# Later takers for the edge counts, one piece of keys per group, and a weight low half ahead of the keys

## What is computed

```python
xn = layernorm(x)
# gnn, two layers; deg_inv = 1 / max(number of edges into a node, 1)
agg = segment_sum(h[src], dst)                       # both layers
h   = relu(xn @ W_self0 + deg_inv * agg(xn) @ W_neigh0 + b0)
gnn = h @ W_self1 + deg_inv * agg(h) @ W_neigh1 + b1
# mix: a linear attention over all nodes
Q, K = elu(xn @ Wq + bq) + 1, elu(xn @ Wk + bk) + 1
KV   = sum(K * (xn @ Wv + bv)); Ksum = sum(K)
mix  = gelu((Q * KV / (Q * Ksum + 1e-6)) @ Wo + bo)
x = x + gnn + mix
x = x + ffn(layernorm(x))                            # quantised, weights (384, 1024)
```

## Time and profile before

| | |
|---|---|
| time, median of 3 runs | 1212.84 us (1212.08 to 1213.51) |
| profiled execution, its own time | 1213.64 us |
| span in its trace | 1211.8 us |
| PE busy | 1157.4 us, 96% |
| DVE busy | 679.4 us, 56% |
| ACT busy | 356.5 us, 29% |
| POOL busy | 393.2 us, 32% |
| scattering indirect DMAs | 160, 2160 ns each on POOL |
| mean granted TensorE clock | 0.986 |

### The profile page before, as it was taken

How to read it: one execution, slowest core, us unless ns; L and a number is a source line. 1 busy time by engine, 2 the same in 40 slices (tenths; PEclk the granted TensorE clock), 3 DMA queues, 4 the chain that set the end, 5 groups by cost and what they waited for, 6 DMA issues and landing times.

```text
span 1211.8 us, 15245 instructions
## 1 busy us (share of the span) xinstructions
PE 1157.4 (96%) x6309; PEld 622.7 (51%) x6309; DVE 679.4 (56%) x1232; ACT 356.5 (29%) x446; POOL 393.2 (32%) x224
## 2 busy tenths in 40 slices
PE   4898999999999999995999999999999999999978
PEld 3554555555555554442444555444444445569934
DVE  7766947658475563335633444656564345582763
ACT  5634333333324323310521112222210012251640
POOL 1266767758677684677400000000000000000000
PEclk8999999999999999998999999999999999999989
DMA  9935344353442439532731034432220080000005
GB/s 259 339 81 140 65 100 99 71 135 50 103 85 37 98 71 311 128 53 58 271 109 39 22 116 162 127 105 88 87 87 35 18 156 1 1 1 1 2 8 161
DMA packets 156151, 117.61 MB, mean 97 GB/s; under 512 B 93401, under 2 KB 132569, under 8 KB 155058
## 3 DMA queue, kind: packets, MB, share of 16 engines
q1 hardware_dynamic: 86744, 103.41, 27.4%
q0 software_dynamic: 69024, 13.07, 8.4%
q10 hardware_dynamic: 314, 0.16, 0.0%
HBM read 90.13 MB, written 21.41 MB: 92 GB/s over the span
## 4 chain that ended last, share of the span: by engine, by line
PE 50%; DMA 21%; issue 14%; POOL 12%; DVE 2%; ACT 1%; SPq 0%; POOLq 0%; ACTq 0%; DVEq 0%
PE ps L1053 25%; DMA at_scratch<-copies,cell 18%; POOL at_scratch L598 12%; PE ps L1085 7%; PE ps L1114 6%; PE ps L1151 6%; PE ps L1181 3%; DMA at_scratch<-zeros 2%; DMA raw<-in_L_mix_Wk_dram 1%; PE ps L1123 1%; PE ps L1101 1%; PE ps L991 0%; DMA parts<-at_scratch 0%; POOL at_scratch L588 0%; DMA key_scratch<-key_r 0%
## 5 line engine op out<-in xcount | busy, mean ns | idle before, releaser
L598 POOL DMA_INDIRECT at_scratch<-copies,cell x160 | 345.6, 2160 | 173.6 <-DMA at_scratch<-copies,cell 93.7
L983 PE MATMUL ps<-xnT,whl 128*128 128x512 f16 (+1 forms) x2160 | 383.3, 340 | 0.0
L983 PEld LDWEIGHTS ps<-xnT,whl 128*128 128x128 f16 x2160 | 211.1, 98 | 169.9 <-issue 1.7
L1053 PE MATMUL ps<-hb,hT 128*128 128x512 f16 x960 | 207.7, 379 | 1.3 <-DVE hT L1516 1.3
L1053 PEld LDWEIGHTS ps<-hb,hT 128*128 128x128 f16 x960 | 93.9, 98 | 114.5 <-DVE hT L1516 1.8
L1053 PE MATMUL ps<-hb,xnT 128*128 128x512 f16 x480 | 105.9, 383 | 12.4 <-DVE hb L1386 12.4
L579 POOL PARTITION_ALL_REDUCE ag_fw<-am_fw x9 | 3.2, 354 | 317.0 <-DVE am_fw L1399 317.0
L1053 PE MATMUL ps<-hb,VT 128*128 128x512 f16 x480 | 103.9, 379 | 1.5 <-ACT S_b L740 1.5
L1085 PE MATMUL ps<-AT,P 125*128 125x512 f16 (+1 forms) x480 | 84.7, 339 | 0.0
L1053 PEld LDWEIGHTS ps<-hb,xnT 128*128 128x128 f16 x480 | 47.3, 99 | 69.9 <-DVE hb L1386 12.9
L1114 PE MATMUL ps<-P,AT 125*128 125x512 f16 x360 | 79.0, 379 | 0.0
(11 more groups left out here) (231 smaller groups left out, 1190.1 us busy)
## 6 DMA issues: line engine op xcount, KB each, us to landing
raw<-in_L_gnn_W_neigh_dram SPq DMA_DIRECT2D x32, 512.0 KB, 5.0
raw<-in_L_gnn_W_self_dram SPq DMA_DIRECT2D x24, 512.0 KB, 5.2
key_b<-key_scratch SPq DMA_DIRECT2D x8, 1250.0 KB, 8.8
raw<-in_L_mix_Wo_dram SPq DMA_DIRECT2D x16, 512.0 KB, 3.9
parts<-at_scratch POOLq DMA_DIRECT2D x20, 312.5 KB, 3.8
at_scratch<-zeros POOLq DMA_DIRECT2D x6, 1020.0 KB, 17.7
x_all<-in_x_dram SPq DMA_DIRECT2D x9, 512.0 KB
x_acc<-in_x_dram SPq DMA_DIRECT2D x9, 512.0 KB
```

The lines of the kernel that those rows point to most:

```text
L598: pool.indirect_dma_start(out=at_scr[c % 2][:, :], out_offset=bass.IndirectOffsetOnAxis(ap=cell[:, c:c + 1], axis=0), in_=copies[:, c:c + ...
L983: mm = pe.matmul(acc_of(c)[:, a:b], whl[:, i, wp, k, :], xnT[:, k, ap, a:b], start=(k == 0 and wp == 0 and ap == 0), stop=(k == KC - 1 and ...
L1053: mm = pe.matmul(half_bank(i), stationary[:, k, ap, t * TP:t * TP + P], hb[:, n % 2, k, wp, :], start=(k == 0 and wp == 0 and ap == 0), st ...
```

## The change

Four places. `PIECE_AT` was (1, 2) for group 0 and then one piece, g + 2, for groups 1 to 5; now group g prepares piece g + 1, for groups 0 to 6. The low half of the fourth chunk of the next group (`chunk_lo(g + 1, 3)`) stood behind the keys and now stands ahead of them. The ten counts were behind tiles 15, 17, 19, 21, 23, 25, 27, 29, 30 and 31 and are now behind 21, 22, 24, 25, 27, 28, 30, 31, 33 and 34. `DEG_TILE` goes from 33 to 36.

```diff
-    PIECE_AT = [(1, 2)] + [(g + 2,) if g + 2 < NPC else () for g in range(1, KC)]
+    PIECE_AT = [(g + 1,) if g + 1 < NPC else () for g in range(KC)]
...
-        DEG_TILE = 33
+        DEG_TILE = 36
...
-        PART_TILE = {i: s for s, i in enumerate((15, 17, 19, 21, 23, 25, 27, 29, 30, 31))}
+        PART_TILE = {i: s for s, i in enumerate((21, 22, 24, 25, 27, 28, 30, 31, 33, 34))}
...
                 v_low(g)
+                if g + 1 < KC:
+                    chunk_lo(g + 1, 3)
                 for p in PIECE_AT[g]:
                     cells(p)
-                if g + 1 < KC:
-                    chunk_lo(g + 1, 3)
-                else:
+                if g + 1 == KC:
                     for j in range(4):
                         job(("half", WO_, 1, j))
```

## The result

| | before | changed |
|---|---|---|
| median | 1212.59 us (4 runs, 1212.08 to 1213.51) | 1199.38 us (4 runs, 1197.6 to 1199.69) |
| ratio | | 0.9887, 95% interval 0.987 to 0.9904 |
| profiled execution, own time | 1213.64 us | 1197.6 us |
| span | 1211.8 us | 1195.8 us |

1.1% faster. Later batches timed the kernel before more often: medians 1213.3 (21 runs, 1209.1 to 1218.4), 1212.6 (11 runs), 1214.4 (13 runs, 1199.4 to 1218.3) and 1212.7 (17 runs, 1205.3 to 1219.8). Of the 11 runs ten lie between 1206.0 and 1215.4 and one, with its clock granted at 0.943 of full speed instead of 0.98 to 0.99, at 1239.98. So the kernel before scatters by 9 us and more, and one of its runs was as fast as the changed kernel; the changed kernel's five runs lie within 2.2 us. The interval above comes from four runs of before that happened to lie within 1.5 us, and is narrower than that scatter allows.

The account below looks back on a forecast made before the run. PE, busy 96% of the span, was taken as the bound, others mattering only where it waits. -7.3 - 14.0 + 6.05 = -15.25 us against 1213.64 gave 1198.4, forecast as 1198.0 (median 0.8 lower), range 1195.0 to 1203.0.

Parts of the forecast that it names:

- The short wait: PE's wait behind chunk 5 for squares of group 2, 5.78 us plus 1.54 slower clock: 7.3 us, all gained.
- The long wait: PE's 12.41 us wait in tile 20 for a low half, plus 1.6 slower clock: 14.0 us, all gained.
- -7.3 - 14.0: Gains behind chunk 5 and in tile 20, added as two separate terms of the sum.
- Pieces later, cost 0: Keys prepared one group later: POOL never stands for keys, its margin of 9 us grows; costed at 0.
- The scatters end as before: POOL's scatters keep their times although keys come later; parts there since 558.75.
- DVE held by POOL: POOL's first six additions, 557 to 571, slow DVE; a count taken at 10.40 us, low halves at 5.04.
- the 9 us of room: DVE frees tile 23 at 588, PE asks at 596.8: holds by 9 us in the worst sum.
- rival B: New wait in tiles 26 to 36 from late banks, tenth count or degree read: 1199 to 1205, chance 0.12.
- The reciprocal, 6.05 us: After tile 39, PE waits 4.55 us for the reciprocal behind tile 38, plus 1.5 slower clock: cost 6.05.
- The clock term: PE's slower clock after the wait for the reciprocal: 1.5 us taken, bounds 0 and 1.7.
- Rival C: Slower: first count waits for later scatters, PE waits from tile 28 if parts land after 579; 1214 or more, chance 0.02.

Follow-up runs that it names:

- experiment 3: Changed kernel with the low half of the fourth chunk back behind the keys, group 0 still with one piece: 1199.41 us.
- Experiment 4: Changed kernel with the old table of pieces of keys (two in group 0), the low half still ahead of them: 1199.46 us.
- experiment 2: Kernel before with only the counts moved to tiles 21 to 34 and DEG_TILE 36: 1206.32 us, ratio 0.9942.
- experiment 7: Kernel before with 100 small memsets on POOL between the last scatter and the first read of the parts: 1231.47 us, ratio 1.0179.
- experiment 8: Changed kernel with 100 small memsets on POOL ahead of the read of the parts: 1199.43 us, ratio 0.9902.
- experiment 10: Kernel before with only the low half of the fourth chunk ahead of the keys, pieces and counts as before: 1209.24 us, ratio 0.9969.
- experiment 1: Changed kernel with counts and DEG_TILE back in their old places, so only keys and low half are moved: 1201.34 us, ratio 0.9918.
- experiment 9: Changed kernel with 200 memsets on POOL ahead of the parts: 1215.3 us; also the changed kernel again, 1199.81, and the kernel before again, 1209.36.
- experiment 5: Changed kernel with every count one tile earlier and DEG_TILE 35: 1191.85 us, ratio 0.9835.
- experiment 6: Changed kernel with the reciprocal in two, 1024 columns behind tile 36 and 226 behind tile 38: 1191.75 us, ratio 0.9832.

## Why the prediction was right, and where its reasoning was not

**The forecast.** 1198.0, likeliest case 1196 to 1200; 1199.38 was measured, and each sign that it named is there: no wait at the sums behind chunk 5, squares ready at 107.1 (forecast "near 108"), no wait in tile 20, one new wait for the reciprocal of 4.53 (4.55).

**The short wait.** Mechanism as argued: the slot of chunk (1,3). Experiments 3 and 4 add that the two edits each suffice; the prediction gave neither by itself a price. Its size of 5.78 was that of one trace: the others that have it show 3.90, 3.99 and 4.87.

**The long wait.** DVE's stand behind tile 15 held tile 20, as experiments 2, 7 and 8 show. But "-7.3 - 14.0" as two gains side by side is wrong for the kernel before, and only right because the change makes both edits. There the path ran through the scatters: the time was the start of the read behind them plus 659 us. The first page said so, in its part on the chain that ended last, with 30% for the scatters and their DMAs; the prediction does not use that part and went by PE's waits alone. A change of group 0 alone would have been forecast 7.3 us faster. The order alone (experiment 10) gives 3.5 and keys and order together (experiment 1) 12.0, both through an earlier end of the scatters. Next to experiment 1 the later counts add only 2 us at the median, for they pay 7.6 at the reciprocal; what they add besides is that the time no longer follows the scatters.

**Pieces later, cost 0.** POOL waited for keys at no scatter after the first, right. "The scatters end as before" was wrong: in the ten traces of kernels without the wait behind chunk 5 they end early enough for a read of the parts at 540 to 555, in the four with it at 550 to 563. The two ranges overlap, so it is the medians of experiments 1 and 10 that carry this. It cost the forecast nothing, since with the counts in their new places PE does not wait for the scatters' end.

**DVE held by POOL.** The dearest low half was given 5.04 us and the dearest count 10.40. Experiment 4 has one of 8.38, the repeat of the changed kernel one of 8.54, and experiment 2 one of 12.34:

```profile
567.80 12.34 DVE L1386 SCALAR_TENSOR_TENSOR hb<-raw,sw,hb 128x1024 f16<-128x1024 f32 x1 [0.35 <-ACT hb L705]
```

The first counts of experiments 8 and 9 took 12.93 and 12.50. So both bounds were too low, and the 9 us of room were less than stated; with parts up to 18 us late none of it reached PE, as experiment 8 shows. Of the Trainium skill's rule (page "SBUF — State Buffer", section "Who interferes with whom"), that the second to issue blocks until the first finishes, the exclusion is borne out, the length is not: a VectorE instruction stood behind five or six GpSimd additions in a row (10.40, 12.34, 12.50, 12.93 us, one addition being 2.3).

**The margins of rival B.** The tenth count and the degree read were said to hold by 1.1 and 0.8 us. They held in every trace; in the changed kernel's first the count was done 1.3 us and the read 0.9 us before PE's column sums began.

**The reciprocal, 6.05 us.** The wait was right to 0.02 us. The clock term was the sum's mis-sized one: 1.5 was taken, with 1.7 as the upper bound, and it was 1.6 in one trace and 2.8 to 3.3 in six. That is enough for the 1.4 us between forecast and median and for the 1.5 us that experiments 5 and 6 gained beyond their expectation. The rows of before had only waits after which the clock rose sooner. The prediction also took 2.4 us for what a measurement of this kernel can tell from nothing; that fits the changed kernel, but not the kernel before, whose runs spread over 20 us.

**Rival C** had the right place and nearly the right point (579 for the parts landing). In experiment 9 the count began at 587.94, as the parts landed, and PE waited 10.1 us from 591.0 on; with the same work behind the parts, PE would begin to wait when they land at about 578 (an estimate from these three numbers).

## What to carry to other kernels

When an engine that others need stands in order behind a long chain, removing a wait ahead of that chain's end gains only what the chain itself ends earlier (here 3.5 or 12 us, where the wait was priced at 7.3). Read the chain that ended last beside the waits, take a wide spread of the times as a hint of it, and make the chain late as a test (18 us cost 17 to 19 before and nothing after). Put the taker of a slow chain late, and then look at what hangs on the taker: here a reciprocal of 8 us ended up with one tile of cover, and splitting it, or moving it one tile earlier, gave 7.6 us more. Where two edits clear the same wait, price them as one.

## What the runs showed of the hardware that was not expected

A wait of PE of 4.53 us costs not one fixed amount for the low clock but 1.6 us or about 3, with the same instructions around it. A wait of 2.33 us early in the kernel did the same on a smaller scale: the 12 matmuls behind it took 4.27 us or, in the changed kernel's first trace, 2.76:

```profile
44.52 2.76 PE L970 MATMUL ps<-xnT,whl 128*128 128x512 f16 x12 [2.33 <-DVE xnT L1251]
```

160 indirect DMAs of 125 elements each, two in flight, ended early enough for a read at 540 in one and only at 563 in another of fourteen traces whose instructions on POOL are the same up to there; the times of the kernel before, which follow them, lie 9 us and more apart. What makes them vary, no run here shows.
